# A four-layer graph network on one core: the last attention sums in a mixed order, and the first layer's norm factor made by GpSimd instead of VectorE and ScalarE's root

## The chip, the core and the metric

The kernel runs on one core of a Trainium2 chip. TensorE multiplies (its weight loads are counted apart, as PEld), VectorE (DVE), ScalarE (ACT) and GpSimd (POOL) do the elementwise work, SyncE (SP) and GpSimd issue transfers. Each engine runs its own queue in order, and engines wait for each other by semaphores. The time is the device time of one execution in microseconds, median of several.

## The reference, cut to what matters

Every layer is x = x + layer(relu(layernorm(x))) on 1250 nodes of 1024 features, with the same 20000 edges in all four.

```python
def _layernorm(x, axis=-1, eps=1e-05):
    m = jnp.mean(x, axis=axis, keepdims=True)
    v = jnp.var(x, axis=axis, keepdims=True)
    return (x - m) / jnp.sqrt(v + eps)
...
h = jnp.maximum(_layernorm(x, axis=-1), 0.0)
x = x + _L0_gnn_ref(...)   # x1 = h @ W1 + b1, then 4 rounds of
                           #   sum over edges of norm * tanh(u[dst] + v[src] + gb) * g[src]
...
# fourth layer, attention:
h = x @ W
e = jnp.exp(-jax.nn.leaky_relu(al[src] + ar[dst], negative_slope=NEG_SLOPE))
rowsum = jax.ops.segment_sum(e, src, num_segments=N)
h_prime = jax.ops.segment_sum(e[:, None] * h[dst], src, num_segments=N)
h_prime = h_prime / (rowsum[:, None] + EPS)
return jax.nn.elu(h_prime)
```

## The kernel before, in words

The nodes are padded to 1280, ten tiles of 128 (T = 10), in five pairs (HT = 5). Every f32 product is made of three: high part times high, high times low, low times high, so each engine that prepares an operand makes a hi and a lo tile.

**First layer.** For each tile VectorE takes mean and variance (`stats_dve`, L495 to L499); for each pair it adds the epsilon (`variance_dve`, L503). ScalarE takes the root (`root_act`, L534), and VectorE makes 1/root with one Newton step (`scale_dve`, L512 to L524): six small instructions, each of which waits for the one ahead, the last being `bias_scale`, the factor by which ScalarE multiplies the bias that it writes into PSUM ahead of the product (`place_bias`, L991). ScalarE multiplies the finished product by `scale0` (`take_x1`, L979). The factor is applied after the product, so that h itself only needs the mean (`h_act`, L539). TensorE transposes h (L563), ScalarE takes its high part (L546), VectorE its low part (L553), and TensorE multiplies by W1 (`x1_pe`, L1885 to L1887).

Between the pieces of this product the edges are counted into a dense matrix, in 25 groups: VectorE makes one-hot tiles `right` and `left` (`cells`, L1340 to L1352), in a ring of three; TensorE multiplies them (`cells_pe`, L1812, L1815); ScalarE copies the sums out. Finished rows are transposed and stored by GpSimd (L841, L844). At the very start GpSimd also splits the edge weights into three parts (L829 to L837), which TensorE picks from (L1777). The order of every engine is written out by hand, step by step. After the last product ScalarE takes the root of the degrees (L1081), loads the table of tanh (L1083), and the four gate rounds begin: ScalarE tanh (L1098), VectorE times the counts (L1498), ScalarE the high part (L1103), VectorE the low part (`mask_lo`, L1503), TensorE 15 matmuls a step (L1962 to L1964).

**Last layer.** The sums over neighbours are made for two tiles of nodes at a time (a group; five groups), in ten steps s, one for each tile of neighbours. VectorE computes the logits, ScalarE their exp, VectorE multiplies by the counts, ScalarE and VectorE split the result into `att_hi[s]` and `att_lo[s]` (the last, L1683, releases TensorE), GpSimd adds up the row sums. `gat_step(s, j, ns)` issues the matmuls of step s for tile j of the group: three for each half n of 512 columns. While a group runs, VectorE and ScalarE also do the output work (divide, elu, residual; L1692 to L1708) of the group before. In the last group (L2073 to L2084) TensorE takes the first tile (j = 0) through all ten steps, then its row sum, then the first half of the second tile's columns through all ten, its row sum, then the other half. Each finished part is taken up by ScalarE and VectorE and stored by SyncE.

Of the kernel before, what the change touches and what calls it, by code (L numbers as in the profile page):

```python
# [24 lines left out]
P = 128  # L25
# [29 lines left out]
HT = T // 2  # L55
# [5 lines left out]
TANH_LEAD = 3  # L61
AL_FIRST = T - 2
LAST_SUMS = (2, 3, 4, 0, 1)
EARLY = 3
LN_STEPS = 3
NORM_STEPS = 4
# [7 lines left out]
def build_program(nc, x, src, dst, edge_weight, w1, b1, gate_w, gate_b, bias1, w2, b2, w3, att, out):  # L74
# [173 lines left out]
    rough = small("rough", [P, 2], F32)  # L248
    square = small("square", [P, 2], F32)
    step = small("step", [P, 2], F32)  # L250
    scale = small("scale", [P, 2], F32)
# [252 lines left out]

    def scale_of(d, i):
        return scale0[:, i, :] if d.n == 0 else scale[:, :]

    def scale_dve(dve, d, i):

        done = NORM_STEPS * d.pairs(i)  # L510
        settled(dve, root_ready, d.pairs(i) + 1)
        nc.vector.reciprocal(rough[:, :], root[:, :]).then_inc(norm_chain0, 1)  # L512
        settled(dve, norm_chain0, done + 1)
        nc.vector.tensor_tensor(square[:, :], rough[:, :], rough[:, :], ALU.mult).then_inc(norm_chain0, 1)
        settled(dve, norm_chain0, done + 2)
        nc.vector.tensor_tensor(square[:, :], square[:, :], variance[:, :], ALU.mult).then_inc(norm_chain0, 1)
        settled(dve, norm_chain0, done + 3)
        nc.vector.tensor_scalar(step[:, :], square[:, :], -0.5, 1.5, ALU.mult, ALU.add).then_inc(norm_chain0, 1)
        settled(dve, norm_chain0, done + 4)
        first = nc.vector.tensor_tensor(scale_of(d, i), rough[:, :], step[:, :], ALU.mult)  # L520
        if d.n == 0:
            first.then_inc(scale_first, 1)
            dve.wait_ge(scale_first, i + 1)
            nc.vector.tensor_tensor(bias_scale[:, i, :], scale0[:, i, :], variance[:, :], ALU.mult).then_inc(scale_ready, 1)  # L524
        elif d.n == 2:
            first.then_inc(scale_first, 1)
            settled(dve, scale_first, HT + i + 1)
            nc.vector.tensor_tensor(scale_dis[:, :], scale[:, :], dis[:, 1, bass.ds(2 * i, 2)], ALU.mult).then_inc(scale_ready, 1)
        else:
            first.then_inc(scale_ready, 1)  # L530

    def root_act(act, d, i):
# [130 lines left out]
    def settled(eng, semaphore, value):  # L663


        eng.wait_ge(semaphore, value)
        eng.sem_inc(settles, 1)
# [135 lines left out]
    def _(pool):  # L803
# [4 lines left out]
                                base=0, channel_multiplier=1).then_inc(consts_done, 1)  # L808
        nc.gpsimd.memset(ones_b[:, :], 1.0).then_inc(consts_done, 1)
        nc.gpsimd.iota(firsts_h[:, :], [[SPAN, WINDOWS]], base=0, channel_multiplier=0,  # L810
                       allow_small_or_imprecise_dtypes=True).then_inc(firsts_done, 1)
# [11 lines left out]
        pool.wait_ge(src_landed, 16)  # L823
        nc.gpsimd.tensor_copy(src_h[0:EDGE_ROWS, :, :], src_rows[0:EDGE_ROWS, :, :]).then_inc(src_ready, 1)
        pool.wait_ge(ew_landed, 16)
        ew_whole = ew_rows[0:EDGE_ROWS, :, :].rearrange("p t c -> p (t c)")
# [11 lines left out]

        for a in range(T):
            pool.wait_ge(count_row_ready, a + 1)  # L840
            pool.dma_start(count_dram[a * P:(a + 1) * P, :], count_row[a % 2][:, :]).then_inc(count_stored[a % 2], 16)  # L841
# [101 lines left out]
    def _(act):  # L943
# [59 lines left out]

        act.wait_ge(consts_done, 2)
        nc.scalar.activation(rden[:, 0, 1:2], zeros[:, 0:1], ACT.Sqrt).then_inc(tanh_idle, 1)
        h_act(act, d, 0, 0)
        transposed_act(act, d, 0, 0)
        root_act(act, d, 0)
        h_act(act, d, 0, 1)
# [24 lines left out]
        for t in range(T):  # L1034
# [6 lines left out]
            if t + 2 < T:  # L1041
                if t % 2 == 1:
                    root_act(act, d, (t + 2) // 2)
                h_act(act, d, (t + 2) // 2, t % 2)
# [225 lines left out]
    def _(dve):  # L1270
# [4 lines left out]
        def rows_before():  # L1275
# [3 lines left out]
            nc.vector.tensor_copy(dst_h[0:EDGE_ROWS, :, :], dst_rows[0:EDGE_ROWS, :, :]).then_inc(dst_chain, 1)  # L1279
            dve.wait_ge(firsts_done, 5)  # L1280
            dve.wait_ge(dst_chain, 1)
# [114 lines left out]
        transposed_dve(dve, d0, 0, 0)  # L1396
        scale_dve(dve, d0, 0)
        for k in range(KT):
# [3 lines left out]
        for t in range(T):  # L1402
# [6 lines left out]
            if t + 2 < T:  # L1409
                stats_dve(dve, d0, (t + 2) // 2, t % 2)  # L1410
                if t % 2 == 1:
                    variance_dve(dve, d0, (t + 2) // 2)
            if t == 0:
                blend_ends()
            if t + 1 < T:
                transposed_dve(dve, d0, (t + 1) // 2, (t + 1) % 2)
            if t + 2 < T and t % 2 == 1:
                scale_dve(dve, d0, (t + 2) // 2)
            if t == 0:
# [341 lines left out]
    def _(pe):  # L1761
# [310 lines left out]

        pe.wait_ge(gat_read, T - GRP - 1)  # L2073
        for s in range(T):
            pe.wait_ge(att_lo_ready, T * (GROUPS - 1) + s + 1)
            gat_step(s, 0, range(2))
        row_sums(0).then_inc(gat_ready, 1)
        pe.wait_ge(gat_read, T - GRP)
        for s in range(T):
            gat_step(s, 1, [0])  # L2080
# [27 lines left out]
```

## Time and profile before

| | us |
|---|---|
| median of 3 runs | 1007.03 (1006.68 to 1008.79) |
| the profiled execution | 1009.05 |
| its span | 1007.5 |
| TensorE matmul busy | 982.6 (98%) |
| VectorE busy | 672.2 (67%) |
| ScalarE busy | 430.4 (43%) |
| GpSimd busy | 126.1 (13%) |
| chain that ended last: TensorE, VectorE | 89%, 8% |

A busy time is the sum of an engine's instruction times, the chain is followed back from the last instruction. In the rows below an idle time in brackets is that of the engine ahead of the instruction, with what ended it; durations of matmuls overlap, so the distance of their starts is what one costs.

### The profile page before, as it was taken

What the parts mean: (1) busy time and instruction counts of PE and PEld (TensorE: products, weight loads), DVE (VectorE), ACT (ScalarE), POOL (GpSimd) and SP (SyncE); (2) the same over time, 40 slices, a digit from 0 to 9 for tenths busy, and PEclk for the clock granted to TensorE, in tenths of its full rate; (3) what the DMA queues carried; (4) which work ended last, traced back from release to release, by engine and by line L of the source; (5) the groups of instructions that cost most, each with busy time, mean ns of one, the idle gap of its engine ahead of it and who ended that gap; (6) DMA issues with size and microseconds to landing.
All of it is one profiled execution on the core that took longest, in us unless ns stands there. A gap on an engine that the chain in (4) does not pass through costs nothing.

```text
span 1007.5 us, 14740 instructions
## 1 busy us (share of the span) xinstructions
PE 982.6 (98%) x5170; PEld 811.6 (81%) x5170; DVE 672.2 (67%) x1251; ACT 430.4 (43%) x655; POOL 126.1 (13%) x160
## 2 busy tenths in 40 slices
PE   6899999999999999999999999999999999999987
PEld 4688888888888888888888888888888888888865
DVE  7888889788777978444494343127356556988883
ACT  5688865554543655221142222242223233354452
POOL 2011400000000010232221000001100000333330
PEclk9999999999999999999999999999999999999998
DMA  7256580000000013755533111322442120111113
GB/s 249 89 182 224 131 258 1 1 22 0 0 21 0 0 23 92 178 202 177 181 108 105 42 42 42 146 105 104 167 153 83 68 99 0 44 65 71 52 70 113
DMA packets 27326, 93.42 MB, mean 93 GB/s; under 512 B 3530, under 2 KB 3530, under 8 KB 27136
## 3 DMA queue, kind: packets, MB, share of 16 engines
q1 hardware_dynamic: 16400, 58.07, 16.6%
q0 software_dynamic: 10880, 34.74, 11.3%
q8 instruction: 29, 0.48, 0.2%
q14 instruction: 17, 0.14, 0.1%
HBM read 64.48 MB, written 33.56 MB: 97 GB/s over the span
## 4 chain that ended last, share of the span: by engine, by line
PE 89%; DVE 8%; issue 2%; ACT 1%; DMA 0%; ACTq 0%; DVEq 0%
PE ps L580 32%; PE ps L2042 12%; PE ps L1962 9%; PE ps L1964 9%; PE ps L1963 9%; PE ps L2015 5%; PE ps L2014 5%; PE ps L563 3%; PE ps L1885 1%; PE ps L1887 1%; PE ps L1886 1%; PE ps L1856 1%; PE ps L1812 1%; PE ps L1815 1%; DVE left L1345 1%
## 5 line engine op out<-in xcount | busy, mean ns | idle before, releaser
L1962 PE MATMUL ps<-g_hi,mask_hi 128*128 128x512 f32 x400 | 157.4, 393 | 1.2 <-DVE mask_lo L1503 1.2
L1964 PE MATMUL ps<-g_hi,mask_lo 128*128 128x512 f32 x400 | 155.8, 390 | 0.0
L1963 PE MATMUL ps<-g_lo,mask_hi 128*128 128x512 f32 x400 | 155.7, 389 | 0.0
L580 PE MATMUL ps<-w_hi,hT_hi 128*128 128x512 f32 x320 | 126.4, 395 | 0.0
L546 ACT ACTIVATE hT_hi<-ps 128x1024 fp32r<-128x1024 f32 x40 | 41.0, 1026 | 198.6 <-PE ps L563 198.6
L580 PE MATMUL ps<-w_lo,hT_hi 128*128 128x512 f32 x320 | 124.7, 390 | 0.0
L2042 PE MATMUL ps<-y_all,att_hi 128*128 128x512 f32 x400 | 112.0, 398 | 4.6 <-DVE att_lo L1683 4.6
L1098 ACT ACTIVATE mask<-ps,v 128x640 f32<-128x640 f32 x80 | 63.5, 794 | 111.7 <-PE ps L1964 52.8
L580 PE MATMUL ps<-w_hi,hT_lo 128*128 128x512 f32 x320 | 98.7, 389 | 0.0
L2042 PEld LDWEIGHTS ps<-y_all,att_hi 128*128 128x128 f32 x400 | 74.8, 191 | 22.3 <-DVE att_lo L1683 6.8
L1962 PEld LDWEIGHTS ps<-g_hi,mask_hi 128*128 128x128 f32 x400 | 75.1, 188 | 19.6 <-DVE mask_lo L1503 3.3
L1964 PEld LDWEIGHTS ps<-g_hi,mask_lo 128*128 128x128 f32 x400 | 75.1, 188 | 15.8
L1963 PEld LDWEIGHTS ps<-g_lo,mask_hi 128*128 128x128 f32 x400 | 75.1, 188 | 15.2
L553 DVE TENSOR_TENSOR hT_lo<-ps,hT_hi 128x1024 fp32r<-128x1024 f32 x40 | 48.9, 1222 | 45.5 <-ACT hT_hi L546 45.5
L1498 DVE TENSOR_TENSOR mask<-mask,countT 128x640 f32<-128x640 f32 x80 | 65.5, 819 | 14.4 <-ACT mask L1098 14.4
L580 PEld LDWEIGHTS ps<-w_hi,hT_lo 128*128 128x128 f32 x320 | 60.1, 188 | 12.8
L580 PEld LDWEIGHTS ps<-w_lo,hT_hi 128*128 128x128 f32 x320 | 60.1, 188 | 11.9
L580 PEld LDWEIGHTS ps<-w_hi,hT_hi 128*128 128x128 f32 x320 | 60.1, 188 | 11.8
L1503 DVE TENSOR_TENSOR mask_lo<-mask,mask_hi 128x640 fp32r<-128x640 f32 x80 | 65.4, 818 | 0.6 <-ACT mask_hi L1103 0.6
L1103 ACT ACTIVATE mask_hi<-mask 128x640 fp32r<-128x640 f32 x80 | 58.8, 735 | 15.3 <-DVE mask L1498 15.0
L2042 PE MATMUL ps<-y_all,att_lo 128*128 128x512 f32 x200 | 64.4, 395 | 0.0
L580 PE MATMUL ps<-wt_hi,hT_hi 128*128 128x512 f32 x160 | 63.3, 396 | 0.0
(197 smaller groups left out, 1831.2 us busy)
## 6 DMA issues: line engine op xcount, KB each, us to landing
xin<-x_after SPq DMA_DIRECT2D x30, 512.0 KB, 3.3
xres<-x_after POOLq DMA_DIRECT2D x20, 512.0 KB, 4.1
x_after<-xres POOLq DMA_DIRECT2D x20, 512.0 KB, 3.0
w_raw<-in_L_gnn_W SPq DMA_DIRECT2D x8, 1024.0 KB, 7.6
x_after<-g POOLq DMA_DIRECT2D x20, 256.0 KB, 7.1
xres<-x_after SPq DMA_DIRECT2D x10, 512.0 KB, 3.3
xin<-in_x SPq DMA_DIRECT2D x9, 512.0 KB, 3.4
out_x<-xres SPq DMA_DIRECT2D x9, 512.0 KB, 2.6
```

What stands on the lines that cost most here:

```text
L553: nc.vector.tensor_tensor(hT_lo[b][:, :, :].rearrange("p k m -> p (k m)"), TRANSPOSED, hT_hi[b][:, :, :].rearrange("p k m -> p (k m)").bit ...
L580: last = nc.tensor.matmul(PRODUCT[d.n][b][:, half * BANK:(half + 1) * BANK], left[:, k, :], right[:, k, half * BANK:(half + 1) * BANK], st ...
L1098: nc.scalar.activation(mask[k][:, :], U_ALL, ACT.Tanh, bias=v[:, s:s + 1]).then_inc(tanh_ready, 1)
L1103: nc.scalar.activation(mask_hi[k][:, :], mask[k][:, :], ACT.Copy).then_inc(mask_hi_ready, 1)
L1498: nc.vector.tensor_tensor(mask[k][:, :], mask[k][:, :], countT[:, s, h * HALF:(h + 1) * HALF], ALU.mult).then_inc(mask_ready, 1)
L1503: nc.vector.tensor_tensor(mask_lo[k][:, :], mask[k][:, :], mask_hi[k][:, :].bitcast(F32), ALU.subtract).then_inc(mask_lo_ready, 1)
L1962: nc.tensor.matmul(SUMS[dd], mask_hi[k][:, cols], g_hi[:, s, :], start=(s == 0), stop=False)
L1963: nc.tensor.matmul(SUMS[dd], mask_hi[k][:, cols], g_lo[:, s, :], start=False, stop=False)
L1964: last = nc.tensor.matmul(SUMS[dd], mask_lo[k][:, cols], g_hi[:, s, :], start=False, stop=(s == T - 1))
L2014: nc.tensor.matmul(out_n, left, y_hi[s][:, n * BANK:(n + 1) * BANK], start=(s == 0), stop=False)
L2015: last = nc.tensor.matmul(out_n, left, y_lo[s][:, n * BANK:(n + 1) * BANK], start=False, stop=(s == T - 1))
L2042: last = nc.tensor.matmul(AGG[j][:, n * BANK:(n + 1) * BANK], left, right[:, n * BANK:(n + 1) * BANK], start=(s == 0 and len(rights) == 2 ...
```

## The change

**The norm factor.** For the first layer alone the factor of a pair is made by GpSimd, in `scale_pool`: a power of -0.5 of the variance, then the same Newton step and the product for the bias, six dependent instructions. VectorE's `scale_dve`, ScalarE's `root_act` and the small first activation with a root are gone from the first layer; the other layers keep them. VectorE waits for the former pair's factor before it overwrites `variance`. `SCALES_AHEAD` sets where the chains stand in GpSimd's queue: pair 0 before the split of the edge weights, pairs 1 to 4 before the stores of count tiles 0, 1, 4 and 7.

**The last sums.** In the last group, the three matmuls of the second tile's first half follow those of the first tile in each of the steps 0 to 6; steps 7 to 9 (`TAIL` = 3) of it come after the first tile's row sum. The rest is as before.

```diff
+SCALES_AHEAD = {0: 1, 1: 2, 4: 3, 7: 4}
+TAIL = 3
...
+    def scale_pool(pool, i):
+
+        done = NORM_STEPS * i
+        pool.wait_ge(var_ready, i + 1)
+        nc.gpsimd.tensor_tensor(rough[:, :], variance[:, :], minus_half[:, :], ALU.pow).then_inc(norm_chain0, 1)
+        pool.wait_ge(norm_chain0, done + 1)
+        nc.gpsimd.tensor_tensor(square[:, :], rough[:, :], rough[:, :], ALU.mult).then_inc(norm_chain0, 1)
+        pool.wait_ge(norm_chain0, done + 2)
+        nc.gpsimd.tensor_tensor(square[:, :], square[:, :], variance[:, :], ALU.mult).then_inc(norm_chain0, 1)
+        pool.wait_ge(norm_chain0, done + 3)
+        nc.gpsimd.tensor_scalar(step[:, :], square[:, :], -0.5, 1.5, ALU.mult, ALU.add).then_inc(norm_chain0, 1)
+        pool.wait_ge(norm_chain0, done + 4)
+        nc.gpsimd.tensor_tensor(scale0[:, i, :], rough[:, :], step[:, :], ALU.mult).then_inc(scale_first, 1)
+        pool.wait_ge(scale_first, i + 1)
+        nc.gpsimd.tensor_tensor(bias_scale[:, i, :], scale0[:, i, :], variance[:, :], ALU.mult).then_inc(scale_ready, 1)
...
         nc.gpsimd.tensor_copy(src_h[0:EDGE_ROWS, :, :], src_rows[0:EDGE_ROWS, :, :]).then_inc(src_ready, 1)
+        pool.wait_ge(firsts_done, 1)
+        scale_pool(pool, 0)
         pool.wait_ge(ew_landed, 16)
...
         for a in range(T):
+            if a in SCALES_AHEAD:
+                scale_pool(pool, SCALES_AHEAD[a])
             pool.wait_ge(count_row_ready, a + 1)
...
-        act.wait_ge(consts_done, 2)
-        nc.scalar.activation(rden[:, 0, 1:2], zeros[:, 0:1], ACT.Sqrt).then_inc(tanh_idle, 1)
         h_act(act, d, 0, 0)
         transposed_act(act, d, 0, 0)
-        root_act(act, d, 0)
...
-                if t % 2 == 1:
-                    root_act(act, d, (t + 2) // 2)
...
-        scale_dve(dve, d0, 0)
...
                 if t % 2 == 1:
+                    dve.wait_ge(scale_ready, (t + 1) // 2)
                     variance_dve(dve, d0, (t + 2) // 2)
...
-            if t + 2 < T and t % 2 == 1:
-                scale_dve(dve, d0, (t + 2) // 2)
...
-        pe.wait_ge(gat_read, T - GRP - 1)
         for s in range(T):
             pe.wait_ge(att_lo_ready, T * (GROUPS - 1) + s + 1)
+            if s == 0:
+                pe.wait_ge(gat_read, T - GRP - 1)
             gat_step(s, 0, range(2))
+            if s == 0:
+                pe.wait_ge(gat_read, T - GRP)
+            if s < T - TAIL:
+                gat_step(s, 1, [0])
         row_sums(0).then_inc(gat_ready, 1)
-        pe.wait_ge(gat_read, T - GRP)
-        for s in range(T):
+        for s in range(T - TAIL, T):
             gat_step(s, 1, [0])
         row_sums(1).then_inc(gat_ready, 1)
```

TensorE's queue about the last group's first row sum, before (`att_hi_121` to `att_hi_130` are the ten steps' tiles; x4 is one tile's both halves, x2 one half):

```order
L2042 MATMUL ps<-y_all,att_hi_129 128x512 x4
L2042 MATMUL ps<-y_all,att_lo_119 128x512 x2
L2042 MATMUL ps<-y_all,att_hi_130 128x512 x4
L2042 MATMUL ps<-y_all,att_lo_120 128x512 x2
L2049 MATMUL ps<-ones,e_sum 128x2
L2042 MATMUL ps<-y_all,att_hi_121 128x512 x2
L2042 MATMUL ps<-y_all,att_lo_111 128x512
```

and now:

```order
L2052 MATMUL ps<-y_all,att_hi_127 128x512 x4
L2052 MATMUL ps<-y_all,att_lo_117 128x512 x2
L2052 MATMUL ps<-y_all,att_hi_127 128x512 x2
L2052 MATMUL ps<-y_all,att_lo_117 128x512
L2052 MATMUL ps<-y_all,att_hi_128 128x512 x4
L2052 MATMUL ps<-y_all,att_lo_118 128x512 x2
L2052 MATMUL ps<-y_all,att_hi_129 128x512 x4
L2052 MATMUL ps<-y_all,att_lo_119 128x512 x2
L2052 MATMUL ps<-y_all,att_hi_130 128x512 x4
L2052 MATMUL ps<-y_all,att_lo_120 128x512 x2
L2059 MATMUL ps<-ones,e_sum 128x2
L2052 MATMUL ps<-y_all,att_hi_128 128x512 x2
```

The second tile's matmuls of steps 0 to 6 (the last of them those of `att_hi_127`) now stand ahead of the row sum, and behind it the second tile begins at step 7.

ScalarE's queue from the end of the branch that is not taken to the first step of the gate rounds (`norm_root` is the root of the degrees, `rden` a dummy activation that brings in the table of tanh), before:

```order
L1058 UNCONDITIONAL_BRANCH
L1081 ACTIVATE norm_root<-norm 128x20
L1083 ACT_TABLE_LOAD
L1083 ACTIVATE rden<-zeros 128x1
L1098 ACTIVATE mask_71<-ps,v 128x640
```

and now:

```order
L1070 UNCONDITIONAL_BRANCH
L1093 ACT_TABLE_LOAD
L1093 ACTIVATE norm_root<-norm 128x20
L1095 ACT_TABLE_LOAD
L1095 ACTIVATE rden<-zeros 128x1
L1110 ACTIVATE mask_71<-ps,v 128x640
```

A second table load now stands ahead of the root of the degrees.

VectorE's queue between the last tile before the counting begins and the first one-hot tile (`complete` is the judgement whether the short way of counting holds), before:

```order
L503 TENSOR_SCALAR variance<-mv 128x2
L553 TENSOR_TENSOR hT_lo_55<-ps,hT_hi_53 128x1024
L512 RECIPROCAL rough<-root 128x2
L514 TENSOR_TENSOR square<-rough 128x2
L516 TENSOR_TENSOR square<-square,variance 128x2
L518 TENSOR_SCALAR step<-square 128x2
L520 TENSOR_TENSOR scale_209<-rough,step 128x2
L524 TENSOR_TENSOR bias_scale<-scale_209,variance 128x2
L1329 TENSOR_SCALAR complete<-ps 128x1
L1340 TENSOR_TENSOR right_144<-iota_b,cell_ids 125x10x50
```

and now:

```order
L506 TENSOR_SCALAR variance<-mv 128x2
L565 TENSOR_TENSOR hT_lo_55<-ps,hT_hi_53 128x1024
L1341 TENSOR_SCALAR complete<-ps 128x1
L1352 TENSOR_TENSOR right_144<-iota_b,cell_ids 125x10x50
L1357 TENSOR_TENSOR left_141<-iota_b,row_ids 125x1280
```

The six instructions of the factor are gone from between.

## Rows read from the trace of the kernel before

**Rows 1.** Instructions in time order, TensorE's end: start, duration, line, idle before.

```profile
966.22 1.17 PE L2042 MATMUL ps<-y_all,att_hi 128*128 128x512 f32 x4
...
981.51 1.20 PE L2042 MATMUL ps<-y_all,att_hi 128*128 128x512 f32 x4 [1.83 <-DVE att_lo L1683]
...
984.65 2.07 PE L2042 MATMUL ps<-y_all,att_hi 128*128 128x512 f32 x4 [1.09 <-DVE att_lo L1683]
...
987.38 0.42 PE L2049 MATMUL ps<-ones,e_sum 128*128 128x2 f32 x2
987.65 1.20 PE L2042 MATMUL ps<-y_all,att_hi 128*128 128x512 f32 x2
...
997.00 0.62 PE L2042 MATMUL ps<-y_all,att_hi 128*128 128x512 f32 x2
...
1002.22 0.39 PE L2042 MATMUL ps<-y_all,att_lo 128*128 128x512 f32 x1
```

**Rows 2.** Waits, 966 to 1008 us: who for whom, total, times, longest.

```profile
ACT elu_neg L1265 <- PE ps L2042: 4.4, 1, 4.4
PE ps L2042 <- DVE att_lo L1683: 4.3, 5, 1.8
```

**Rows 3.** In time order, VectorE, then GpSimd, at 970 to 980 us.

```profile
977.89 1.21 DVE L1704 SCALAR_TENSOR_TENSOR elu_neg<-elu_neg,xres 128x1024 f32<-128x1024 f32 x1
...
970.48 0.73 POOL L929 TENSOR_TENSOR e_part<-e_part,att_e 128x256 f32<-128x256 f32 x1 [1.22 <-DVE att_e L1678]
...
977.91 1.79 POOL L929 TENSOR_TENSOR e_part<-e_part,att_e 128x256 f32<-128x256 f32 x1 [0.89 <-DVE att_e L1678]
```

**Rows 4.** By window: length, busy by engine, granted clock, DMA share, GB/s.

```profile
44.40:46.40 2.00, 1.87 (x39) 1.90 (x40) 2.00 (x5) 0.76 (x2) 0.00 (x0) 1.00 0.03 8
985.00:987.00 2.00, 2.00 (x6) 1.52 (x6) 0.00 (x0) 0.00 (x0) 0.00 (x0) 0.50 0.92 270
```

**Rows 5.** In time order, TensorE's waits for one-hot tiles in the first layer.

```profile
34.63 0.21 PE L1812 MATMUL ps<-right,left 125*128 125x90 bf16 x1 [1.78 <-DVE right L1352]
...
44.53 0.20 PE L1812 MATMUL ps<-right,left 125*128 125x90 bf16 x1 [2.52 <-DVE right L1352]
...
70.66 0.20 PE L1812 MATMUL ps<-right,left 125*128 125x90 bf16 x1 [0.74 <-DVE right L1352]
```

**Rows 6.** In time order, VectorE in the first layer.

```profile
19.42 1.28 DVE L495 BATCH_NORM_STATS2 stats<-xin 128x6 f32<-128x512 f32 x2
...
31.16 0.15 DVE L512 RECIPROCAL rough<-root 128x2 f32<-128x2 f32 x1
...
32.67 0.15 DVE L1329 TENSOR_SCALAR complete<-ps 128x1 int32<-128x1 f32 x1
```

**Rows 7.** Load of the third x tile, and all five of line 690 by then.

```profile
9.64 0.33 SPq L690 DMA_DIRECT2D xin<-in_x  x1
...
DMA to landing us min/median/max: 3.2/3.4/9.0
```

**Rows 8.** In time order, GpSimd at the start.

```profile
2.14 0.14 POOL L812 IOTA row_no<- 128x4 f32 x1
...
10.83 0.39 POOL L829 CAST ew_part<-ew_rows 80x250 bf16<-80x250 f32 x1 [2.52 <-DMA ew_rows<-in_edge_weight]
11.31 0.66 POOL L831 TENSOR_TENSOR ew_rest<-ew_rows,ew_part 80x250 f32<-80x250 f32 x1
```

**Rows 9.** In time order at 119 to 125 us: ScalarE, VectorE, TensorE.

```profile
118.89 1.28 ACT L1083 ACT_TABLE_LOAD   x1
120.19 0.20 ACT L1083 ACTIVATE rden<-zeros 128x1 f32<-128x1 bf16 x1
120.89 0.80 ACT L1098 ACTIVATE mask<-ps,v 128x640 f32<-128x640 f32 x1 [0.49 <-issue]
...
123.64 0.82 DVE L1503 TENSOR_TENSOR mask_lo<-mask,mask_hi 128x640 fp32r<-128x640 f32 x1 [0.36 <-ACT mask_hi L1103]
...
124.61 0.47 PE L1962 MATMUL ps<-g_hi,mask_hi 128*128 128x512 f32 x1
```

**Rows 10.** By line and shape, GpSimd's longest arithmetic: busy and mean, idle before.

```profile
L880 POOL TENSOR_TENSOR xres<-xres,row_all 128x1024 f32<-128x1024 f32 x10 | 24.7, 2469 | 45.6 <-DVE xres L1587 45.6
```

More of the change, by code:

```diff
@@ L249, in build_program @@
     square = small("square", [P, 2], F32)
+    minus_half = small("minus_half", [P, 2], F32)
     step = small("step", [P, 2], F32)
@@ L503, in variance_dve @@
         nc.vector.tensor_scalar(variance[:, :], mv[:, :, 1], EPS_LN, None, ALU.add).then_inc(var_ready, 1)
-    def scale_of(d, i):
-        return scale0[:, i, :] if d.n == 0 else scale[:, :]
     def scale_dve(dve, d, i):
         done = NORM_STEPS * d.pairs(i)
-        settled(dve, root_ready, d.pairs(i) + 1)
+        settled(dve, root_ready, d.pairs(i) - HT + 1)
         nc.vector.reciprocal(rough[:, :], root[:, :]).then_inc(norm_chain0, 1)
@@ L519, in scale_dve @@
         settled(dve, norm_chain0, done + 4)
[L520 to L525, printed above, removed]
+        first = nc.vector.tensor_tensor(scale[:, :], rough[:, :], step[:, :], ALU.mult)
+        if d.n == 2:
             first.then_inc(scale_first, 1)
@@ L809, in _ @@
         nc.gpsimd.memset(ones_b[:, :], 1.0).then_inc(consts_done, 1)
+        nc.gpsimd.memset(minus_half[:, :], -0.5).then_inc(firsts_done, 1)
         nc.gpsimd.iota(firsts_h[:, :], [[SPAN, WINDOWS]], base=0, channel_multiplier=0,
@@ L1279, in rows_before @@
             nc.vector.tensor_copy(dst_h[0:EDGE_ROWS, :, :], dst_rows[0:EDGE_ROWS, :, :]).then_inc(dst_chain, 1)
-            dve.wait_ge(firsts_done, 5)
+            dve.wait_ge(firsts_done, 6)
             dve.wait_ge(dst_chain, 1)
```

## The prediction

> **What bounds the kernel.** I read the chain of waits, then the waits of the last attention group and of the first 125 us, then the instructions there in order of time. Between those two places TensorE issues one 128x512 matmul after another, so the edits can only act at the two ends of the program.
>
> At the end TensorE is paced by VectorE. From 966.22 us it runs the last group's ten steps for its first tile, six matmuls a step, and waits five times for att_lo, 4.3 us together [rows 1, 2]. They come late because VectorE does the previous group's output work between them (1.21 us at 977.89 is a piece of it [rows 3]); the last lets TensorE go at 984.65 [rows 1]. Behind it TensorE still has 66 matmuls: 6 of this step, 30 for the first 512 columns of the second tile, 30 for the rest; the last starts at 1002.22 and lasts 0.39, so 984.65 to 1002.61 is 17.96 us [rows 1]. A part of that ran at half speed: in 985 to 987 us the granted clock was 0.50, that is 1.2 of 2.4 GHz, after an idle 1.83 and an idle 1.09 us, and six matmuls took 984.65 to 987.38, 0.455 us each [rows 1, 4]. At full clock 997.00 to 1002.22 holds 23 matmul starts: 0.227 us each [rows 1]. Then one chain of ScalarE, VectorE and a store follows, whatever came before.
>
> At the start, TensorE waits for VectorE's one-hot tiles three times: 1.78 us at 34.63, 2.52 at 44.53, 0.74 at 70.66, 5.04 in all, and no more in the node sums after that [rows 5].
>
> **The last sums.** No matmul is added or removed; 21 (seven steps of three) are moved ahead, from behind the last att_lo to a place where TensorE waited. VectorE and ScalarE make att_lo without anything from TensorE's last group, so the last one still comes at 984.65. Before it TensorE now has 7 x 9 + 2 x 6 = 75 matmuls: 966.22 + 75 x 0.227 = 983.2, so it is free in time and idles 1.4 us once. Behind it stand 66 - 21 = 45: 10.2 us, and 0.5 for the two row sums (987.38 to 987.65 is 0.27 for one [rows 1]): 10.7. Saving 17.96 - 10.7 = 7.2 us; of it 4.8 is the 21 moved matmuls, the rest the half clock that I expect not to come. For that speaks that 2.52 us of waiting at 44.53 came with a granted clock of 1.00 in the two microseconds after [rows 4]. If the clock falls all the same, the matmuls from 984.65 on pay what they paid before, about 2.4, and 4.8 is left: the range of this term is 4.6 to 7.4. The first tile's sum is complete at about 986.1 instead of 987.6, the second tile's first half at 988.4, and the last half's at 995.4. ScalarE waited 4.4 us for this last sum before [rows 2]. Now the output work of the first tile, 1.5 us earlier, is met by that of the second's first half, 7 us earlier, so most of the 4.4 goes, but I expect the last chain to stay the last.
>
> **The norm factor on VectorE.** Each of the five pairs took VectorE six small instructions, 31.16 to 32.67: 1.5 us [rows 6]. What it is worth is what TensorE waits for behind it.
> - Pair 0: VectorE starts its next tile's statistics at 19.42, but that tile's load was issued at 9.64 and such loads took up to 9.0 us to land, so not before 18.6 [rows 6, 7]. I take 0.8; ends 0 and 1.5.
> - Pair 1: straight ahead of the first one-hot tiles: 1.5. The two together, 2.3, come off the waits of 1.78 and 2.52, which hold them.
> - Pair 2 lies before the wait of 0.74 at 70.66 and is longer than it: 0.74.
> - Pairs 3 and 4: TensorE does not wait behind them: 0.
> Sum 3.0; top end 3.8.
>
> **The same factor on GpSimd.** Six dependent instructions on 128x2. No row has a power, nor any arithmetic on so small a tile. A 128x4 iota took 0.14 us, an 80x250 tensor_tensor 0.66 [rows 8]; with 0.09 between dependent ones (10.83 + 0.39 to 11.31 [rows 8]) a chain costs 1.4 to 4.5 us. I take 2, five instructions near the lower row and a power near the upper. ScalarE needs the results for the bias it places. The first chain also stands ahead of the split of the edge weights, which began at 10.83 and is waited for by TensorE's picks. A delay of the picks of up to about 2 us is hidden by the wait at 44.53, which would still be 2.1 without it. GpSimd's stores of counts come after chains 2 to 4, and nobody waits for them soon. VectorE's added wait for scale_ready before it overwrites variance is for a chain half a dozen microseconds older: 0. So this costs 0 at 2 us a chain.
>
> GpSimd and VectorE get in each other's way: e_part's sum took 0.73 at 970.48 and 1.79 at 977.91, beside VectorE's two-input 128x1024 operation [rows 3]. The Trainium skill's page "SBUF — State Buffer", "Who interferes with whom", says that a VectorE instruction with two SBUF inputs and a GpSimd one that reads SBUF exclude each other for the whole instruction; the trace agrees, and by that rule every link of chains 2 to 4 can stand behind a one-hot instruction, and also hold one up. That is the second rival below.
>
> **ScalarE's root.** Five roots of 0.2 us go, and the first table load, at the start with nothing waiting, stays (now ahead of the first Relu). But the root of the degrees, once per kernel, stays, and no root table is loaded any more when it comes: the order shows a new table load in front of it, and the tanh's behind it. Before, only the tanh's stood there: 1.28 us at 118.89; then ScalarE had 0.49 us of slack before the first tanh at 120.89 [rows 9]. So the first tanh is 1.28 - 0.49 = 0.8 us later, then mask_hi, then mask_lo(0), which started at 123.64, took 0.82 and was at once used by TensorE at 124.61 [rows 9]. There is no slack left, and VectorE then has no spare time for ten steps: +0.8. Ends 0 and 1.3.
>
> The Trainium skill, "ScalarE: Activation LUTs", "What ACT_TABLE_LOAD costs", gives 1283 ns for the load and 1380 more for a drain, 2.66 us for a switch. The trace has the load's 1.28, but the next activation starts 1.30 after it began [rows 9], without a drain. By the page the term would be 2.66 - 0.49 = 2.2, and the whole 1.4 us worse.
>
> **Sum.** -7.2 - 3.0 + 0.8 = -9.4 us. The profiled execution took 1009.05 us (span 1007.50 and 1.55 around it) and would take 999.6; it was 2.0 above the median of 1007.03. Against the median: 997.6 us. With the terms' good ends 1007.0 - 7.4 - 3.8 = 995.8; with 4.6 at the end, nothing in the first layer and 1.3 for the table: 1003.7.
>
> **Rivals.**
> 1. *The clock falls at the end* in the one idle stretch left, as it did before 985. For: the fall before came with no single wait over 1.83 us. Against: the long wait at 44.53. Then 2.4 more: 1000.0. Chance 0.15.
> 2. *The first layer gives nothing.* The GpSimd chains, held up by VectorE's two-input instructions, come at 4 us or more, ScalarE stands at the bias, and the cells behind it come late; or VectorE loses in lock-outs what it was relieved of. For: 1.79 against 0.73 us [rows 3]; chain 2 begins when GpSimd has just issued two stores. Against: TensorE was not waiting at those places. Then only the table and the end count: 1007.0 - 7.2 + 0.8 = 1000.6. Chance 0.2.
> 3. *Slower than before: the power is slow.* If GpSimd works a power as a long routine or loads it first, a chain of C us delays the edge weights' picks by C - 1.4, and later each bias by about C - 3. At C = 3.5 the relief is still there; the last sums' 7.2 and the 3.0 are used up from C of about 6.5 on (5 + 4 x 3.5 = 19 of waits, of which TensorE's own work behind the bias hides about half). At C = 8: (6.6 - 2.1) + 4 x 2.5 = 14.5, less 6.4 of net gain (7.2 - 0.8) = +8: 1015. For: no row prices it. Against: the longest GpSimd arithmetic in the trace is 2.5 us for 1024 columns [rows 10]. Chance 0.04.
> 4. *The change does not do what it says at the end.* The order shows 75 matmuls ahead of the first row sum and the same sums; but a wait inside the first step (for ScalarE's copy of the previous group's second tile) could hold all that follows. For: the wait is new at this place. Against: six matmuls, 1.4 us, stand ahead of it. Then there is no gain but the first layer's: 1007.0 - 3.0 + 0.8 = 1004.8. Chance 0.03.
>
> **Chances.** The forecast has 0.58. Within 0.2% (2 us, what a measurement of this kernel can tell from no change) is what rivals 2 and 4 reach together in part, 0.03; slower 0.03; faster 0.94. The range leaves out rival 3 and the best tenth: 995.2 to 1001.8.
>
> **What the profile would show.** TensorE: one wait of about 1.4 us for the last att_lo and none before; last att matmul at about 993 of a shorter span; granted clock 1.00 there. Waits for one-hot tiles: about 2 us in all, not 5. The dis factors and first mask_lo 1.3 and 0.8 later against TensorE, with an idle of some 0.8 us ahead of the first gate sum. GpSimd's chain: 2 us, the power under 0.7. Wrong it would be if a GpSimd power takes over 3 us, if ScalarE idles for bias_scale, or if the end's sums still run at 0.45 us a matmul.

## The result, and the profile after

The changed kernel takes 1001.58 us (median of 5 runs, 1001.28 to 1003.81), the kernel before took 1007.17 beside it (5 runs, 1006.68 to 1008.79): ratio 0.9944, 95% interval 0.9931 to 0.9957. The gain is 5.6 us, where 9.4 were forecast. The profiled executions differ by more: 1009.05 and 1001.58, 7.5 us. Those 1.9 us between the two ways of counting turn out to be half of the error. Two of the five runs of the changed kernel took 1002.52 and 1003.81, and left no trace.

TensorE's end, in time order, of the kernel after (answers to rows 1):

```profile
965.63 1.17 PE L2052 MATMUL ps<-y_all,att_hi 128*128 128x512 f32 x4
...
984.06 1.19 PE L2052 MATMUL ps<-y_all,att_hi 128*128 128x512 f32 x4 [1.12 <-DVE att_lo L1693]
...
985.56 0.28 PE L2059 MATMUL ps<-ones,e_sum 128*128 128x2 f32 x2
...
994.66 0.39 PE L2052 MATMUL ps<-y_all,att_lo 128*128 128x512 f32 x1
```

Its waits from 966 to 1000 us (rows 2):

```profile
ACT elu_neg L1277 <- PE ps L2052: 1.1, 1, 1.1
PE ps L2052 <- DVE att_lo L1693: 1.1, 1, 1.1
```

This is the end that the prediction drew: one wait instead of five, and from its end to the last matmul's 984.06 to 995.05, 10.99 us, where the kernel before took 17.96 [rows 1]. ScalarE waits 1.1 us for the last sum instead of 4.4 [rows 2]. Six matmuls from 984.06 to 985.56 are 0.25 us each, not 0.455.

GpSimd at the start, in time order (rows 8), then what TensorE and VectorE do about it (rows 5 and 6):

```profile
9.22 0.73 POOL L532 TENSOR_TENSOR rough<-variance,minus_half 128x2 f32<-128x2 f32 x1 [1.72 <-DVE variance L506]
10.03 0.19 POOL L534 TENSOR_TENSOR square<-rough 128x2 f32<-128x2 f32 x1
...
11.27 0.39 POOL L844 CAST ew_part<-ew_rows 80x250 bf16<-80x250 f32 x1
...
12.46 2.00 POOL L848 CAST ew_part<-ew_rest 80x250 bf16<-80x250 f32 x1
14.54 0.95 POOL L850 TENSOR_TENSOR ew_rest<-ew_rest,ew_part 80x250 f32<-80x250 f32 x1
15.55 0.73 POOL L852 CAST ew_part<-ew_rest 80x250 bf16<-80x250 f32 x1
```

```profile
16.34 2.76 PE L1787 MATMUL ps<-picks,ew_part 80*125 80x500 bf16 x6 [2.48 <-POOL ew_part L852]
...
43.31 0.20 PE L1822 MATMUL ps<-right,left 125*128 125x90 bf16 x1 [1.73 <-DVE right L1364]
...
69.30 0.20 PE L1822 MATMUL ps<-right,left 125*128 125x90 bf16 x1 [0.75 <-ACT weights_sd L972]
```

```profile
12.93 5.71 DVE L1411 TENSOR_TENSOR w_lo<-w_raw,w_hi 128x512 fp32r<-128x512 f32 x8
18.56 1.27 DVE L498 BATCH_NORM_STATS2 stats<-xin 128x6 f32<-128x512 f32 x2
...
31.45 0.15 DVE L1341 TENSOR_SCALAR complete<-ps 128x1 int32<-128x1 f32 x1
```

The power costs 0.73 us and the whole chain 9.22 to 11.32, 2.1, as taken. But the split of the edge weights behind it, which began only 0.44 us later than before (11.27 against 10.83 [rows 8]), ends at 16.28 and not at 13.57, 2.7 us later, because VectorE's eight w_lo subtractions now lie beside it (experiment 4): the same cast takes 0.39 alone and 2.00 there. What brought them together is mostly VectorE's relief: without the six instructions of the factor it starts the subtractions at 12.93, where it was 14.32 before:

```profile
14.32 1.29 DVE L1400 TENSOR_TENSOR w_lo<-w_raw,w_hi 128x512 fp32r<-128x512 f32 x2
```

The split of before, shifted by the 0.44 us alone, would have ended at 14.01, ahead of that (worked out, not run). By the records the cast of 12.46 begins ahead of the first subtraction and alone would have ended at 12.85; GpSimd's times in a trace are rough, and it is experiment 4 that ties the two together.

TensorE has a new wait of 2.48 us; the one-hot tiles (just behind `complete`) start 1.22 us earlier than in [rows 6], not 2.3; the wait at 34.63 is gone, that at 44.53 shrank from 2.52 to 1.73, and the third stayed, now put down to ScalarE.

What the late picks did to the first one-hot tile, in the kernel after, ScalarE's bias and VectorE's last tile ahead of `complete`, and the same two before:

```profile
26.76 0.69 ACT L1008 ACTIVATE ps<-b_all,bias_scale 128x512 f32<-128x512 f32 x1 [3.85 <-PE ps L1872]
...
30.31 1.22 DVE L565 TENSOR_TENSOR hT_lo<-ps,hT_hi 128x1024 fp32r<-128x1024 f32 x1 [1.32 <-ACT hT_hi L558]
```

```profile
24.81 0.69 ACT L991 ACTIVATE ps<-b_all,bias_scale 128x512 f32<-128x512 f32 x1 [2.38 <-PE ps L1862]
...
30.02 1.23 DVE L553 TENSOR_TENSOR hT_lo<-ps,hT_hi 128x1024 fp32r<-128x1024 f32 x1 [0.68 <-ACT hT_hi L546]
```

ScalarE waits for TensorE until 26.76 instead of 24.81, and VectorE then waits 1.32 us for ScalarE's high part instead of 0.68. So VectorE, which was 0.86 us ahead at its second tile's statistics (18.56 against 19.42 [rows 6]), is 0.29 behind at 30.31; pair 1's 1.5 us on top of that makes the 1.22.

ScalarE and TensorE at 117 to 124 us (rows 9):

```profile
117.19 1.28 ACT L1093 ACT_TABLE_LOAD   x1
118.48 0.22 ACT L1093 ACTIVATE norm_root<-norm 128x20 f32<-128x20 f32 x1
118.72 1.28 ACT L1095 ACT_TABLE_LOAD   x1
...
123.92 0.47 PE L1972 MATMUL ps<-g_hi,mask_hi 128*128 128x512 f32 x1 [0.88 <-DVE mask_lo L1513]
```

ScalarE's last copy ahead of these stands at 116.48 (118.08 before, 1.6 later), but TensorE's first gate sum is only 0.69 ahead of [rows 9]: the second table load stands between (0.8 us of it by experiment 3).

### The profile page after: what moved, and what is told of

Same layout as the page of the kernel before. It is cut to its first block, busy times and chain, and to the rows that moved or that the text cites. A ratio compares the mean times of both kernels' runs of the same rounds, so it can differ in the third digit from the quotient of the medians.

```text
span 1000.0 us, 14720 instructions
## 1 busy us (share of the span) xinstructions
PE 977.4 (98%) x5170; PEld 809.6 (81%) x5170; DVE 668.7 (67%) x1221; ACT 430.9 (43%) x650; POOL 140.4 (14%) x191
## 4 chain that ended last, share of the span: by engine, by line
PE 91%; DVE 5%; ACT 2%; issue 1%; POOL 1%; DMA 0%; ACTq 0%; DVEq 0%; POOLq 0%
PE ps L592 32%; PE ps L2052 11%; PE ps L1972 9%; PE ps L1974 9%; PE ps L1973 9%; PE ps L2025 5%; PE ps L2024 5%; PE ps L575 3%; PE ps L1895 1%; PE ps L1897 1%; PE ps L1896 1%; PE ps L1866 1%; PE ps L1822 1%; PE ps L1825 1%; PE ps L1838 1%
## 5 line engine op out<-in xcount | busy, mean ns | idle before, releaser
L2052 PE MATMUL ps<-y_all,att_hi 128*128 128x512 f32 x400 | 110.0, 393 | 1.5 <-DVE att_lo L1693 1.5
```

The lines of the kernel that those rows point to most:

```text
L2052: last = nc.tensor.matmul(AGG[j][:, n * BANK:(n + 1) * BANK], left, right[:, n * BANK:(n + 1) * BANK], start=(s == 0 and len(rights) == 2 ...
```

## Experiments

Each is the changed kernel with the edit shown (shortened), unless it says otherwise; medians of five runs (twelve and eleven for the second and the tenth). The kernel before, run beside them, took 1007.19 us in the first four, 1008.42 in the next four, 1007.07 in the next three and 1007.26 in the last. The changed kernel itself was not run again beside them: where a time is compared with its 1001.58, the five runs of above (1001.28 to 1003.81) are meant, and a difference of half a microsecond between medians is not told from their spread.

**1. The last sums alone** (the kernel before, with this):

```
+TAIL = 3
 for s in range(T):
     ...
     gat_step(s, 0, range(2))
+    if s < T - TAIL:
+        gat_step(s, 1, [0])
```

> The kernel before with the mixed order of the last sums and nothing else; its norm factors still come from ScalarE's root and VectorE. Theory A: the order alone brings nearly all of the gain, since from the start of the last group's waits (984.06) to the last matmul's end it took 10.99 us after the change and 17.96 before; expected 6.9 us less in the trace, and in the medians between 5.0 and 6.9, so 1000.3 to 1002.2 (the changed kernel: 1001.6). Theory B: the first layer's part brings 2.2 or more and the order only some 3.5; then this kernel takes about 1003.7. In the trace of the last group TensorE has one wait of about 1.1 us for an att_lo tile instead of many, and the granted clock stays at 1.00 to the end.

1002.28 us (1002.01 to 1002.67), ratio 0.9945 (0.9931 to 0.9960): theory A's mechanism, 0.1 us above its range. The order alone brings 4.9 of the 5.6. That leaves 0.7 for the first layer's part, the same as the 0.69 between the first gate sums of the two traces, but the medians don't prove it: the ratios (0.9945 and 0.9944) are the same. From the last wait's end, 984.86, to the last matmul's, 995.85, it is 10.99 us, as in the changed kernel, at a granted clock of 1.00. In its trace TensorE's clock falls in the first layer; the window, and TensorE's waits around it:

```profile
36.00:38.00 2.00, 2.00 (x11) 1.24 (x10) 2.00 (x4) 1.47 (x3) 0.00 (x0) 0.57 0.29 98
```

```profile
34.64 0.21 PE L1813 MATMUL ps<-right,left 125*128 125x90 bf16 x1 [1.78 <-DVE right L1353]
...
44.55 0.20 PE L1813 MATMUL ps<-right,left 125*128 125x90 bf16 x1 [1.09 <-DVE right L1353]
```

It costs nothing here: the wait behind it, 2.52 us in [rows 5], took it up and is 1.09, and the first gate sum stands at 124.64, where it was 124.61.

**2. The norm factor alone** (the end as in the kernel before):

> The changed kernel with the old order of the last sums, so the first layer's part alone. Theory A (the gain at the first one-hot tile, 1.22 us, less a table load of 0.8 on the path and the third wait that stayed): 0 to 0.6 us less than before, about 1006.8. Theory B (the forecast's own sum for these parts): 2.2 less, 1005.0. Theory C (what is missing in the medians, 5.6 against 7.5 in the traces, is lost in the first layer): 1 us more than before, about 1008. Its end should look as the kernel before's: waits for att_lo, and a granted clock near 0.50 in places.

1007.22 us, but from 1006.29 to 1011.00; ratio 0.9998 (0.9987 to 1.0010). Theory B (2.2 less) falls; A's 0 to 0.6 can't be told from nothing in the medians. The spread is the finding. Five of its runs have spans of 1004.8 to 1005.2 at a mean granted clock of 1.0, three have 1007.6 to 1009.5 at 0.994. Its profiled execution is one of the first kind; TensorE's end in time order, and windows (columns as in rows 4):

```profile
984.11 1.19 PE L2051 MATMUL ps<-y_all,att_hi 128*128 128x512 f32 x4 [1.49 <-DVE att_lo L1692]
...
999.47 0.39 PE L2051 MATMUL ps<-y_all,att_lo 128*128 128x512 f32 x1
```

```profile
984.00:986.00 2.00, 1.89 (x9) 1.63 (x10) 0.05 (x1) 0.08 (x2) 0.00 (x0) 1.00 0.84 213
986.00:988.00 2.00, 2.00 (x10) 1.63 (x10) 1.07 (x3) 1.11 (x3) 0.00 (x0) 1.00 0.77 311
```

The old order at full clock takes 15.75 us from 984.11 to 999.86. So of the 17.96 of [rows 1], 2.2 was a clock that had fallen, and in this run, after waits as long (1.81 and 1.49), it had not, against what I expected of this end. The order itself is worth 15.75 - 10.99 = 4.76. Run against run at full clock: 1006.3 to 1001.5, 4.8.

**3. Sqrt's table loaded at the start:**

```
+act.wait_ge(consts_done, 2)
+activation(rden[:, 0, 1:2], zeros[:, 0:1], ACT.Sqrt)...
 h_act(act, d, 0, 0)
```

> The changed kernel, with a Sqrt of one column put back at ScalarE's very start, whose result nobody reads. It is there for its table alone: Sqrt's table is then in before the degree norm's root. Theory A: the load of 1.28 us at 117.19 stood on the path for 0.8 us; it goes, and the kernel takes 0.8 us less than the changed one (range 0.5 to 1.0), about 1000.8. Theory B: the load lay beside VectorE's work there, or one load comes elsewhere on the path; no difference. In the trace the root starts about 117.2 rather than 118.5, and TensorE's wait for mask_lo ends 0.8 to 1.3 earlier.

1000.79 us (1000.58 to 1001.23), ratio 0.9931 (0.9917 to 0.9946): 0.8 less, as theory A said. The load in front of norm_root is gone, and norm_root stands at 117.24 (118.48). The table term was right.

**4. VectorE keeps off GpSimd's split:**

```
+dve.wait_ge(parts_chain, 5)
 for k in range(KT):
     dve.wait_ge(w_hi_ready, k + 1)
     ... w1_lo
```

> The changed kernel, with VectorE's eight w1_lo subtractions waiting until GpSimd has split the edge weights into their three parts. Theory A: GpSimd's split was late (16.3 instead of 13.6) because these eight instructions, back to back with two operands in SBUF, kept it from its memory port; without them beside it the first cast takes 0.39 us instead of 2.00, the split ends about 14.0, TensorE's wait for it (2.48 us) shrinks to some 0.2 to 0.5, and the first one-hot tile starts up to 1 us earlier, if w1_lo's own delay (they end 14.0 + 5.7 = 19.7, and TensorE wants the first at about 20.5 less the earlier picks) does not take it back; 0 to 1.0 us less than the changed kernel. Theory B: GpSimd is slow there for another reason (its own instructions after a power), and the cast keeps its 2 us; the time is 1 us more.

1002.72 us (1002.02 to 1002.85), 1.1 slower than the changed kernel. GpSimd's and VectorE's rows, then TensorE's, then the window behind TensorE's last one:

```profile
12.88 0.39 POOL L848 CAST ew_part<-ew_rest 80x250 bf16<-80x250 f32 x1
```

```profile
14.46 4.91 DVE L1412 TENSOR_TENSOR w_lo<-w_raw,w_hi 128x512 fp32r<-128x512 f32 x8 [1.75 <-POOL ew_part L852]
```

```profile
14.48 2.76 PE L1788 MATMUL ps<-picks,ew_part 80*125 80x500 bf16 x6 [0.92 <-POOL ew_part L852]
...
42.88 0.20 PE L1823 MATMUL ps<-right,left 125*128 125x90 bf16 x1 [2.51 <-DVE right L1364]
```

```profile
44.00:46.00 2.00, 2.00 (x12) 1.98 (x10) 2.00 (x5) 1.25 (x3) 0.00 (x0) 0.50 0.00 0
```

The lock-out is shown: the cast of 2.00 us takes 0.39 when nothing lies beside it, and VectorE's eight take 4.91 instead of 5.71. TensorE's new wait shrank to 0.92, and both the first one-hot tile (`complete` at 31.02) and the matmul at 42.88 come 0.43 us earlier than in the changed kernel. But TensorE's wait ahead of 42.88 grew from 1.73 to 2.51, and this time the clock fell to 0.50 behind it. From there to ScalarE's copy (111.80 here, 110.65 there) it took 68.92 us instead of 67.34, 1.6 more. Neither theory had that: B's number, 1 us more, came out, but its reason did not.

**5. The degrees' norm by GpSimd's power too:**

```
+pool: tensor_tensor(dis, norm, minus_halves, ALU.pow)   # 128x20
-act:  activation(norm_root, norm, ACT.Sqrt)
-dve:  reciprocal(dis, norm_root)
 act:  activation(rden, zeros, ACT.Tanh)   # moved to ScalarE's start
```

> The changed kernel, with the degree norm treated as the first layer's factor was: GpSimd raises the 20 columns of degrees to the power -0.5 and VectorE's Newton step refines it; ScalarE's root and VectorE's reciprocal go, and Tanh's table is loaded once at ScalarE's start. The root's path was 3.31 us of VectorE's wait, up to 118.73, and no load of 1.28 us is left behind the last product. Theory A (a power costs its 0.72 us whatever its size): dis is ready some 2 us earlier, and 0.8 to 1.5 us are won on the changed kernel, so 1000.1 to 1000.8. Theory B (the 0.52 us that a power of two columns takes beyond another operation on them, 0.26 a column, grows with the columns): the power takes 5.4 us and ends near 121, 2 us later than the reciprocal did; 1.5 to 2.5 us slower than the changed kernel, about 1003.5.

1003.10 us (1002.44 to 1003.72), 1.5 slower than the changed kernel: near theory B, though no table load is left behind the last product. In the trace, a run of 1002.44 at a mean granted clock of 1.0, TensorE's last group begins 0.9 later (966.54); the three runs at 0.997 and 0.998 lift the median. GpSimd's row, then VectorE's:

```profile
116.30 3.57 POOL L882 TENSOR_TENSOR dis<-norm,minus_halves 128x20 f32<-128x20 f32 x1 [0.67 <-issue]
```

```profile
119.90 0.18 DVE L1497 TENSOR_TENSOR norm_step<-dis 128x20 f32<-128x20 f32 x1 [4.70 <-POOL dis L882]
```

A power grows with the columns: 0.73 for 2, 3.57 for 20, so by an estimate from these two 0.16 us a column beside 0.4 fixed (theory B had 0.26). For twenty columns it doesn't pay here.

**6. Transposes of tile 1 ahead of the edge-weight picks:**

```
+transpose_pe(pe, d0, 0, 1)
 pe.wait_ge(parts_chain, 5)
 ... picks of the three parts
 ...
-    if t + 1 < T:
+    if 0 < t < T - 1:
         transpose_pe(...)
```

> The changed kernel, with TensorE's eight transposes of tile 1 moved from behind the edge-weight picks into the 2.48 us that it waits for them. Theory A: 1.1 us of work comes out of the path to the first one-hot tile; ScalarE's bias and widening start 1 us earlier and the one-hot tiles 0.5 to 1.0 us earlier; about 0.5 to 0.8 us less than the changed kernel. Theory B (from the run in which w1_lo waited): what TensorE gains early it spends waiting for a one-hot tile near 43 us; if that wait grows beyond 2 us the granted clock falls to 0.50 behind it, as there, and the kernel is 0.5 to 1.2 us slower than the changed one. Theory C: VectorE's queue holds the one-hot tiles where they were; no difference.

1001.98 us (1001.00 to 1002.16): no gain, and theory B's mechanism. Where the granted clock was 1.0 the spans were 999.5 and 999.9 (the changed kernel: 1000.0), where it was 0.997 or 0.998 they were 1000.5 and 1000.6. TensorE's row, then the windows behind it:

```profile
42.40 0.20 PE L1823 MATMUL ps<-right,left 125*128 125x90 bf16 x1 [2.52 <-DVE right L1364]
```

```profile
42.00:44.00 2.00, 1.60 (x32) 1.63 (x33) 2.00 (x4) 0.49 (x2) 0.00 (x0) 0.72 0.03 8
44.00:46.00 2.00, 2.00 (x10) 1.90 (x9) 2.00 (x5) 1.36 (x3) 0.00 (x0) 0.50 0.00 0
```

**7. TAIL = 1.**

> The changed kernel with TAIL = 1: six more matmuls of the second part (6 x 0.227 = 1.36 us) stand ahead of the last att_lo tile's wait (1.12 us). Theory A: TensorE ends 1.12 us earlier, but the first row sum comes 0.24 us later and with it VectorE's chain of the two other output parts, which then ends at 995.43 instead of 995.19, so that the last part starts at 995.43 instead of 995.88: 0.45 us less than the changed kernel. Theory B: only TensorE's end counts, 1.1 less. Theory C: the end had no slack on the other engines, no difference.

1001.48 us (1000.91 to 1002.85). **8. TAIL = 2.**

> The changed kernel with TAIL = 2: three more matmuls (0.68 us) ahead of the last att_lo tile's wait, of which 0.44 us is then left, and the first row sum stays where it was. Theory A: TensorE ends 0.68 us earlier, and VectorE is free at 995.19, 0.69 us before it took the last part up: 0.68 us less than the changed kernel, more than with TAIL = 1 (0.45). Theory B: only TensorE's end counts; less than with TAIL = 1 by 0.44.

1001.49 us (1000.96 to 1002.51). In the medians neither shows. In the traces both do: from the start of the last group's matmuls to the end of VectorE's last instruction it is 965.63 to 997.29 in the changed kernel, 31.66 us, 31.03 with TAIL = 1 (967.56 to 998.59) and 31.05 with TAIL = 2 (965.65 to 996.70). Both save 0.6, between the 0.45 and 0.68 of the two theories A; that TAIL = 2 saves more than TAIL = 1 did not show, and theories B (more with TAIL = 1) fall. With TAIL = 1 nothing is left of TensorE's wait, but VectorE's chain then sets the end in both. The medians don't show it; what differs from run to run at the start is larger. In the profiled run of TAIL = 1 the lock-out caught GpSimd's split one instruction earlier (the subtraction of L846, 2.09 us instead of 0.66), and TensorE's picks came at 17.30 (16.34 in the changed kernel); the last group began 1.9 us later. GpSimd's row there:

```profile
12.52 2.09 POOL L846 TENSOR_TENSOR ew_rest<-ew_rows,ew_part 80x250 f32<-80x250 f32 x1
```

**9. Transposes as in 6, and the wait filled:**

```
 def cells_pe(g):
+    if g == 3:
+        for _ in range(5):
+            matmul(ps[:, 2*BANK:3*BANK], zeros, zeros[:, 0:1].to_broadcast([P, BANK]))
     pe.wait_ge(cells_ready, g + 1)
```

> The changed kernel with the transposes of tile 1 moved ahead (as in the run before), and five matmuls of zeros (5 x 0.22 us) on TensorE ahead of the fourth group of cells, where it waited 2.52 us for a one-hot tile and its granted clock then fell to 0.50 for some 4 us. Theory A: that fall, and it alone, ate the gain of the earlier transposes (the run before: 1002.0 us, its two runs at a granted clock of 1.0 had spans of 999.5 and 999.9, the changed kernel 1000.0). With the wait cut to some 1.4 us the clock stays at 1.00 in all runs, and the kernel takes 0.5 to 0.8 us less than the changed one's 1001.5: 1000.7 to 1001.1. Theory B: the clock falls all the same, in other places or there; 1002.0 as before.

1000.97 us (1000.78 to 1001.25), ratio 0.9933 (0.9920 to 0.9947): theory A, inside its 1000.7 to 1001.1. TensorE's rows:

```profile
39.97 1.03 PE L1817 MATMUL ps<-zeros 128*128 128x512 bf16 x4
...
42.41 0.20 PE L1827 MATMUL ps<-right,left 125*128 125x90 bf16 x1 [1.41 <-DVE right L1365]
```

(The row shows four of the five.) The one-hot tile comes at the same moment as in 6, 42.40; the granted clock is 1.00 from there to the end of TensorE's work. 1.0 us less than in 6 (which ran apart from it, on another chip), 0.6 less than the changed kernel.

**10. The kernel before, its last waits filled** with 3, 6 and 5 matmuls of zeros ahead of the sixth, ninth and tenth att_lo tile:

> The kernel before, with matmuls of zeros on TensorE in the old order of its last sums: 3, 6 and 5 of 0.22 us ahead of the sixth, ninth and tenth att_lo tile of the last group, where it waited 0.97, 1.81 and 1.49 us. They lie inside those waits and bring nothing by themselves. Theory A: the 17.96 us from the last wait's end to the last matmul's end in the trace of the kernel before held 2.2 us of a fallen clock (15.75 in the run of the old order in which the clock stayed at 1.00), and what makes its times spread up to 1010.7 is this fall. Filled, all runs lie within 0.5 us of 1006.8, and the changed kernel stands 4.8 + 0.6 below it. Theory B: the fall doesn't come from these waits; the times spread as those of the kernel before, with some at 1008 to 1010.

1006.98 us (1006.66 to 1008.27), ratio 0.9997 (0.9988 to 1.0006). Windows of its profiled execution:

```profile
44.00:46.00 2.00, 1.56 (x31) 1.59 (x32) 2.00 (x4) 0.30 (x1) 0.00 (x0) 0.53 0.03 8
...
984.00:986.00 2.00, 1.59 (x8) 0.62 (x7) 1.73 (x2) 0.00 (x0) 0.32 (x1) 1.00 0.15 53
986.00:988.00 2.00, 2.00 (x11) 1.65 (x11) 0.17 (x2) 0.41 (x2) 0.00 (x0) 1.00 0.94 246
```

Half of theory A. The end keeps its clock: from the last wait's end, 985.78, to the last matmul's, 1001.53, is 15.75 us, the same as in 2, though the waits for att_lo were shorter only by what the zeros filled. The runs do not all lie at 1006.8, though: six have spans of 1005.1 to 1005.4 and five 1006.5 to 1006.8, and the profiled one, of the second kind, has its fall at 44 to 48 us, behind the first layer's wait of 2.52 us (ScalarE's copy at 112.02 before stands at 113.21, 1.2 later). The mean granted clock doesn't tell the two kinds apart (0.998 and 0.999), and only the profiled run left a trace, so that the other four of the second kind had the same fall is inferred. Of the 15 runs of the kernel before beside it, five have spans of 1007.2 to 1007.4, some 1.8 us above its others (clock 0.996 or 0.997); they have no match here.

**11. Sqrt at the start and TAIL = 2 together:**

> The changed kernel with both edits that helped: a Sqrt of one column at ScalarE's start (0.8 us less) and TAIL = 2 (0.68 us off TensorE's last wait). If they add up and nothing else takes their place: 1.2 to 1.5 us less than the changed kernel, 1000.1 to 1000.3. If TAIL = 2 brings nothing in the median (its own run: 1001.5), 1000.8.

1001.01 us (999.61 to 1001.71). Less gain than the sum; the median lies near the 1000.8 of the second expectation. One run had a span of 998.1 at clock 1.0 (999.61, under the 1000.1 to 1000.3 expected); three had 999.5 or 999.6 at 0.997 or 0.998, and one 1000.1 at 1.0. In the profiled one of these GpSimd's split was early (picks at 15.04), TensorE's wait at 42.92 became 2.39 us and the clock fell to 0.57.

**12. All that helped:** the Sqrt, TAIL = 2, the transposes and the filling.

> The changed kernel with the four edits together: a Sqrt of one column at ScalarE's start, TAIL = 2, the transposes of tile 1 ahead of the edge-weight picks, and the five matmuls of zeros ahead of the fourth group of cells, which keep the granted clock at 1.00 there. If their gains add up on the run with transposes and filling (1000.97): 0.8 less for the table load and 0.68 less for the end, so 999.5 (range 999.2 to 1000.0), with a spread under 1 us. If the clock falls behind the 1.4 us wait near 42 us in part of the runs, 1000.5 and a spread of over 1 us.

999.40 us (998.70 to 999.64), ratio 0.9916 (0.9903 to 0.9930) to the kernel before: 2.2 us under the changed kernel, the best version found, and inside the expected 999.2 to 1000.0 with a spread under 1 us. Its waits, in time order:

```profile
42.24 0.20 PE L1829 MATMUL ps<-right,left 125*128 125x90 bf16 x1 [1.42 <-DVE right L1367]
...
981.90 1.21 PE L2059 MATMUL ps<-y_all,att_hi 128*128 128x512 f32 x4 [0.46 <-DVE att_lo L1696]
```

## Why the prediction was right, and where not

Faster, and within its range of 995.2 to 1001.8; but the likeliest value, 997.6, is 4.0 us too low. The median lies 0.2 us inside the upper end, with two of its five runs outside, so luck had a share in the range holding.

**The last sums: the mechanism right, the size 2.4 too large for the median.** Forecast 7.2, and in the two traces 6.97 went; alone it brings 4.9 (experiment 1). The 21 moved matmuls are 4.76 (forecast 4.8). The other 2.4 was the fallen clock in the profiled execution of before, real there (2.2), but, by their spans, absent in more than half of its runs: of 41 beside the first eleven experiments 22 had spans under 1006 us, where the profiled one had 1007.5.

**The step that failed is the last one, "it was 2.0 above the median of 1007.03. Against the median: 997.6".** The sum had taken the fallen clock out as a gain, and the step took the same time out again as the profile's distance from the median. The profiled execution was 2.0 above the median because of that fall: with the end filled, those runs disappear (experiment 10), and the old order at full clock ends 2.2 us sooner (experiment 2). The profile's own forecast, 999.6 against 1001.58, was 2.0 off. So of the 3.8 us by which the gain fell short, 2.0 is this step, about 1.5 the norm factor below, and 0.2 the last sums (10.99 us and not 10.7).

**The norm factor off VectorE: 3.0 forecast, about 1.5 found** (ScalarE's copies at 112.02 and 118.08 before stand at 110.65 and 116.48). Pairs 0 and 1 brought 1.22 at the first one-hot tile instead of 2.3: pair 0's 0.8 was there at 18.56 and was lost by 30.31, to the wait for ScalarE. Pair 2's 0.74 brought nothing: in the trace of before VectorE's tile (69.74 + 0.77) and ScalarE's copy (69.98 + 0.53) were both ready at 70.51, and TensorE needs both (its wait is put down to the first in [rows 5], to the second in the kernel after). A wait is worth no more than the gap to the second-latest of what it waits for, and I had not looked for that.

**The factor on GpSimd: cost 0 forecast at 2 us a chain.** The first two chains take 2.1, as taken, and the power 0.73; the other three take 3.3, 3.2 and 3.7, and ScalarE idles 0.77 us for the last one's bias_scale, at 107.50. That was one of the signs of being wrong; TensorE does not wait behind it. What was missed is what it displaced. I allowed the picks up to 2 us of delay, hidden behind the wait at 44.53; the delay is 2.7, as VectorE's w_lo, 1.4 us earlier, came to lie beside the split. And it was not hidden: TensorE's product, then ScalarE's bias and copies, then VectorE's one-hot tiles come behind the picks, so both sides of that wait moved. Rival 2 named the lock-out, at the later chains, and priced it at the whole gain; half was lost, and at the split. Experiment 4 shows the lock-out (0.39 against 2.00) and a part of its price: up to 42.88, ahead of the fall of the clock, its edit brought 0.43 us, with VectorE's own waiting already paid. In experiment 11's trace, where the split ended at 14.98 by itself, `complete` stood at 31.06, 0.39 earlier than in the changed kernel. These are single traces.

The Trainium skill's page "SBUF — State Buffer", "Who interferes with whom", has the rule that a VectorE instruction with two inputs in SBUF and a GpSimd instruction that reads SBUF shut each other out. The runs agree, with the 0.39 and 2.00 us above; the cast lasted longer than any one of the eight VectorE instructions (0.68 us in the median, 1.11 the longest), so it seems to have been passed over more than once, which no run shows by itself.

**The table load: right.** +0.8 forecast, 0.79 in experiment 3. The next activation starts 1.29 us after each of the two loads began, so nothing but the load stands between.

**Sum by what was found:** -4.76 - 1.5 + 0.8 = -5.5, against 5.6 measured. The match is closer than the runs can bear out: 0.7 for the first layer comes from single traces, and experiment 2 has it at nothing, from 1.3 us less to 1.0 more.

Rival 1 did not happen in the profiled execution of the changed kernel (1.00 to the end); rival 3 fell with the power's 0.73 us, and rival 4 with the single wait at 984.06.

**Open:** why a wait of 2.5 us near 43 us is followed by a fallen clock in some executions and not in others (1.00 in [rows 4], 0.50 to 0.53 in experiments 4, 6 and 10) no run tells. Of the first layer's missing 1.5 us, pair 2's 0.7 and the loss of pair 0's 0.8 are accounted for by the traces; how much of the latter the split's delay alone cost is shown only by the 0.43 and 0.39 of experiments 4 and 11.

## What to carry to other kernels

When a profiled execution lies above the median, find what in it is the excess before you scale: here it was a clock fall at the very place being improved, and it was counted twice. Work moved to an idle engine can cost more than its own time: it pushes that engine's next work later and pulls the relieved engine's next work earlier, and here the two then lay beside each other (0.44 and 1.39 us). Look at what comes to overlap. A microsecond won ahead of TensorE may only lengthen its next wait, and the clock may fall behind that; matmuls of zeros inside the wait made the gain stay (experiments 6 and 9).

## What the runs showed of the hardware

- GpSimd's power on 128 partitions: 0.73 us for 2 columns, 3.57 for 20; a multiplication of 2 columns 0.19. The links behind the power, 0.19 us each at the start, took up to 0.72 in the last chain, at 106.69; what lay beside them was not examined.
- GpSimd's 80x250 cast of f32 to bf16: 0.39 us with nothing of VectorE's beside it, 2.00 beside a row of subtractions with two inputs in SBUF.
- The granted clock at one and the same wait is a matter of the single run: the wait of 2.52 us was followed by a granted clock of 1.00 in [rows 4] and of 0.53 in experiment 10. The spans of experiment 10 fall into two groups, 1005.1 to 1005.4 and 1006.5 to 1006.8, those of experiment 6 into 999.5 to 999.9 (clock 1.0) and 1000.5 to 1000.6 (0.997 or 0.998).
- With zeros in a wait of 2.52 us, 1.41 of it left idle, five runs lay within 0.5 us of each other (mean granted clock 0.999 or 1.0).
